# Block transposes on VectorE and a round trip through memory in place of TensorE's transposes, and squares laid out with the summed index innermost, in a Mamba-2 mixer with feed-forward

## The chip, the cores and the metric

The kernel runs on one core of a Trainium2 chip. The metric is the device time of one execution in microseconds, given as the median of several runs. The engines are TensorE (PE, matmuls; PEld is its weight load), VectorE (DVE), ScalarE (ACT), GpSimd (POOL) and SyncE (SP), which in this kernel issues nearly all DMAs. Each engine works through its own queue in order and waits at semaphores.

## The reference

The mixer works on 2 sequences of 512 tokens with 512 channels. The input is projected to a gate, to 8192 channels of heads (128 heads of 64), to B and C (8 groups of 128 states) and to a step size dt for each head. The channels pass a short convolution over 4 tokens and a SiLU. Cut to what matters:

```python
hs = hBC[..., :INTER].reshape(b, s, H, P)
xch = (hs * dt[..., None]).reshape(b, nc, CHUNK, H, P)
Y_diag = jnp.einsum('bzlhn,bzshn,bhzls,bzshp->bzlhp', Cc, Bc, L, xch)
states = jnp.einsum('bzlhn,bhzl,bzlhp->bzhpn', Bc, decay_states, xch)
...
Y = (Y_diag + Y_off).reshape(b, s, H, P) + hs * D[None, None, :, None]
g = y * jax.nn.silu(gate)
gg = g.reshape(b, s, G, INTER // G)
var = jnp.mean(gg * gg, axis=-1, keepdims=True)
gg = gg * jax.lax.rsqrt(var + EPS)
```

An output projection, a residual with layer norm, and a small feed-forward part with low-rank terms and a second layer norm follow. All values are float32.

## The kernel before

**Tiling.** The 1024 tokens are 8 chunks `c` of 128, four to a sequence (`CPB`). The 128 heads are cut into 16 units of 8 heads, 512 channels; a group `g` of B and C has two units, `e` = 0 and 1. A step is (g, e, c), and there are 128. `body(g, last)` on every engine loops over `e` and `c`; the lists `WORK` and `LOOP_TILES` say which weight tiles are projected in which step, 1 to 3 a step and with one or two batches (12 matmuls each), so the next unit's channels are made while this one is worked on. Large operands are split into a high and a low part (`w_hi`, `w_lo`; `xd_hi`, `xd_lo`; `g_hi`, `g_lo`) and multiplied in three float32r matmuls.

**One step.** The channels `hs` have the channel on the partitions. The recurrence needs them with the token on the partitions. So TensorE's `front` (L526) makes four 128x128 transposes into PSUM `p_hid`, and VectorE's `front` (L1210) multiplies by dt into `xdt`. TensorE multiplies `xdt` by the decay matrix into `p_yd` (L690, 8 heads). Right behind `p_yd` stands the front of the next step, then the state update `p_st` (L700 to L702), which needs `xd_hi` and `xd_lo` of the next chunk: GpSimd's `decay_hidden` (L1052, L1054, L1056) makes them from `xdt`. Then comes the output projection of the step before (L562 to L564), which needs its `g_hi` (ACT) and `g_lo` (VectorE).

VectorE adds `y` = `p_yd` + `dh` (L1375), GpSimd multiplies it by the gate (`gate_y`, L1144), ACT squares it into `ysq` (L980) and makes `g_hi`; VectorE sums the squares over the unit's four channel tiles (L1423, L1432), makes `g_lo`, and then `eac` (`scale_off`, L1258) for the next step, which GpSimd adds into `dh` (L1092).

**Queues.** The order in each queue is written out by hand. GpSimd's step is: add `dh`, scale the state (L1097), then for its first tile `split_lo` (`w_lo`, L1034), `gate_y`, `rs`, `skip` (L1063), `decay_hidden` of the next step; then `split_lo` of further tiles. SP's step is: `eac`, `decay`, then for each tile of the step a `raw` load (L388) of the tile four places ahead, which waits until the slot's last content has been split, that is for `w_lo` (and `w_hi`) of the tile two places ahead.

## Time and profile before

| | |
|---|---|
| Median of 3 runs | 1598.37 us (1598.18 to 1598.73) |
| Span of the profiled execution | 1596.2 us |
| TensorE busy | 1577.7 us, 99% |
| VectorE busy | 1347.6 us, 84% |
| ACT busy | 1230.8 us, 77% |
| GpSimd busy | 1224.1 us, 77% |
| DMA | 178.69 MB, mean 112 GB/s |

The span is that of one profiled execution, from the first to the last instruction; the runs' time also holds what lies around it, and the median stands 2.2 us above the span. Busy shares are averages over the whole span; whether an engine sets the time is read from what the others wait for. A matmul's recorded duration overlaps the next one's, so TensorE's times are best read from start to start.

### The profile page before, as it was taken

The numbers are of one execution on the slowest core, as the hardware profiler recorded it, in microseconds if no ns is written. First come the engines' busy times: TensorE is split into PE (matmuls) and PEld (weight loads), VectorE is DVE, ScalarE is ACT, GpSimd is POOL, SyncE is SP. The second block draws the span as 40 slices with busy tenths as digits, with TensorE's granted clock in tenths as the row PEclk, the third lists the DMA queues.
The fourth block names the chain that finished last, engine by engine and source line by source line (L and its number), as shares of the span: only waits on it lengthen the run. The fifth ranks groups of instructions, "written<-read, shape, count | busy, mean of one in ns | idle before, by whom it ended". The sixth has DMA issues, their size and how long they took to land.

```text
span 1596.2 us, 27397 instructions
## 1 busy us (share of the span) xinstructions
PE 1577.7 (99%) x9112; PEld 1299.6 (81%) x9112; DVE 1347.6 (84%) x1878; ACT 1230.8 (77%) x2391; POOL 1224.1 (77%) x1013
## 2 busy tenths in 40 slices
PE   8999999999999999999999999999999999999998
PEld 6878888888888888888888888888888888888865
DVE  6787898879979799787988889887998879978797
ACT  5888778886778877787877877878777886878864
POOL 4578788787797868878687787878688786787864
PEclk9999999999999999999999999999999999999999
DMA  3643424233242322333234332433334333342411
GB/s 116 200 157 108 130 83 153 87 115 108 87 145 96 123 100 100 129 100 109 87 115 140 99 123 74 131 118 92 116 101 136 102 102 106 100 149 77 142 60 60
DMA packets 88156, 178.69 MB, mean 112 GB/s; under 512 B 16592, under 2 KB 20688, under 8 KB 87760
## 3 DMA queue, kind: packets, MB, share of 16 engines
q1 hardware_dynamic: 87008, 176.77, 34.2%
q8 instruction: 74, 1.21, 0.3%
q14 instruction: 66, 0.54, 0.1%
q10 hardware_dynamic: 1008, 0.17, 0.1%
HBM read 172.17 MB, written 4.72 MB: 111 GB/s over the span
## 4 chain that ended last, share of the span: by engine, by line
PE 94%; DVE 1%; POOL 1%; ACT 1%; issue 1%; DMA 0%; SPq 0%; POOLq 0%; DVEq 0%; ACTq 0%
PE proj L514 16%; PE proj L516 16%; PE proj L515 16%; PE p_yd L690 8%; PE p_out L562 7%; PE p_out L564 7%; PE p_out L563 7%; PE p_st L571 5%; PE p_hid L526 4%; PE proj L626 2%; PE p_st L702 1%; PE p_st L700 1%; PE p_st L701 1%; PE p_misc L537 1%; PE p_misc L583 0%
## 5 line engine op out<-in xcount | busy, mean ns | idle before, releaser
L514 PE MATMUL proj<-x_hi,w_hi 128*128 128x512 f32 x1160 | 462.0, 398 | 7.6 <-DVE x_lo L1323 7.0
L515 PE MATMUL proj<-x_lo,w_hi 128*128 128x512 f32 x1160 | 452.9, 390 | 0.0
L516 PE MATMUL proj<-x_hi,w_lo 128*128 128x512 f32 x1160 | 452.9, 390 | 0.0
L1034 POOL TENSOR_TENSOR w_lo<-raw,w_hi 128x512 fp32r<-128x512 f32 x209 | 284.2, 1364 | 101.8 <-ACT w_hi L754 99.3
L1198 DVE SCALAR_TENSOR_TENSOR hs<-proj,uch,hs 128x511 f32<-128x511 f32 (+2 forms) x384 | 285.4, 743 | 42.4 <-ACT hs L781 37.5
L842 ACT ACTIVATE decay<-decay,tok 128x128 f32<-128x128 f32 x1024 | 312.4, 391 | 0.0
L514 PEld LDWEIGHTS proj<-x_hi,w_hi 128*128 128x128 f32 x1160 | 218.8, 189 | 53.2 <-issue 11.2
L516 PEld LDWEIGHTS proj<-x_hi,w_lo 128*128 128x128 f32 x1160 | 218.3, 188 | 46.2
L515 PEld LDWEIGHTS proj<-x_lo,w_hi 128*128 128x128 f32 x1160 | 218.9, 189 | 42.2
L1227 DVE TENSOR_TENSOR decay<-decay,cb 128x1024 f32<-128x1024 f32 x128 | 199.0, 1555 | 56.0 <-ACT decay L860 54.3
L1092 POOL TENSOR_TENSOR dh<-dh,eac 128x512 f32<-128x512 f32 x96 | 127.2, 1325 | 144.0 <-DVE eac L1258 140.3
L1144 POOL TENSOR_TENSOR y<-y,gate 128x512 f32<-128x512 f32 x128 | 180.0, 1406 | 50.3 <-DVE y L1375 50.3
L562 PE MATMUL p_out<-wo_hi,g_hi 128*128 128x512 f32 x512 | 203.6, 398 | 3.3 <-DVE g_lo L1251 3.3
L564 PE MATMUL p_out<-wo_hi,g_lo 128*128 128x512 f32 x512 | 200.1, 391 | 0.0
L563 PE MATMUL p_out<-wo_lo,g_hi 128*128 128x512 f32 x512 | 199.5, 390 | 0.0
L781 ACT ACTIVATE hs<-proj,uch 128x512 f32<-128x512 f32 x128 | 98.6, 773 | 78.8 <-PE proj L516 77.9
L980 ACT ACTIVATE ysq<-y 128x512 f32<-128x512 f32 x128 | 79.9, 624 | 98.8 <-POOL y L1144 98.8
L1375 DVE TENSOR_TENSOR y<-p_yd,dh 128x512 f32<-128x512 f32 x128 | 87.7, 685 | 68.7 <-PE p_yd L690 41.5
L1063 POOL TENSOR_TENSOR dh<-hs,uch 128x512 f32<-128x512 f32 x122 | 145.1, 1189 | 0.0
L754 ACT ACTIVATE w_hi<-raw 128x512 fp32r<-128x512 f32 x197 | 122.8, 623 | 28.2 <-PE proj L516 28.2
L1056 POOL TENSOR_TENSOR xd_lo<-xd,xd_hi 128x512 fp32r<-128x512 f32 x96 | 135.9, 1416 | 7.7
L690 PE MATMUL p_yd<-decay,xdt 128*64 128x128 f32 x2048 | 140.1, 279 | 0.0
(139 smaller groups left out, 3037.6 us busy)
## 6 DMA issues: line engine op xcount, KB each, us to landing
decay<-acum_d SPq DMA_DIRECT2D x128, 512.0 KB, 4.4
raw<-w_t SPq DMA_DIRECT2D x209, 256.0 KB, 2.9
eac<-eacum_d SPq DMA_DIRECT2D x192, 128.0 KB, 3.0
wo_raw<-wo_t SPq DMA_DIRECT2D x32, 256.0 KB, 4.0
c_new<-wo_t SPq DMA_DIRECT2D x32, 256.0 KB, 4.2
hs<-x_t SPq DMA_DIRECT2D x8, 256.0 KB, 5.7
acc<-x_tok SPq DMA_DIRECT2D x8, 256.0 KB, 3.1
out<-acc SPq DMA_DIRECT2D x8, 256.0 KB, 2.0
```

What stands on the lines that cost most here:

```text
L514: nc.tensor.matmul(dst[:], w_hi[:, ws, k, :], x_hi[:, k, cols], start=(k == 0), stop=False)
L515: nc.tensor.matmul(dst[:], w_hi[:, ws, k, :], x_lo[:, k, cols], start=False, stop=False)
L516: mm = nc.tensor.matmul(dst[:], w_lo[:, ws, k, :], x_hi[:, k, cols], start=False, stop=(k == KC - 1))
L562: nc.tensor.matmul(p_out[:], g_hi[:, j, :], wo_hi[:, j, :], start=(j == 0), stop=False)
L563: nc.tensor.matmul(p_out[:], g_hi[:, j, :], wo_lo[:, j, :], start=False, stop=False)
L564: mm = nc.tensor.matmul(p_out[:], g_lo[:, j, :], wo_hi[:, j, :], start=False, stop=(j == UT - 1))
L690: mm = nc.tensor.matmul(p_yd[(h % 2) * HD:(h % 2 + 1) * HD, h // 2, :], xdt[:, h, :], decay[:, dslot(c), h, :], start=True, stop=True)
L842: ins = nc.scalar.activation(decay[:, dslot(c), h, :], decay[:, dslot(c), h, :], ACT.Relu, scale=-1.0, bias=tok[:, e, 0, c, h:h + 1])
L1034: nc.gpsimd.tensor_tensor(w_lo[:, s].rearrange("p a b -> p (a b)"), raw[:, s, :], w_hi[:, s].rearrange("p a b -> p (a b)").bitcast(F32), A ...
L1144: nc.gpsimd.tensor_tensor(y[:], y[:], gate[:, c // CPB, :, (c % CPB) * P:(c % CPB + 1) * P], ALU.mult).then_inc(gated, 1)
L1198: nc.vector.scalar_tensor_tensor(out=dst[:, shift:], in0=src[:, :SEQ - shift], scalar=w, in1=dst[:, shift:], op0=ALU.mult, op1=ALU.add).th ...
L1227: nc.vector.tensor_tensor(decay[:, dslot(c)], decay[:, dslot(c)], bcast(cb[:, c, :], 1, UH), ALU.mult).then_inc(mix_ready, 1)
```

## The change

For the chunks 1 to 7 of a unit the tokens are turned in another way. VectorE's `turn_blocks` transposes the sixteen 32x32 blocks of each partition quadrant (a 32x32 block transpose stays within its 32 partitions) into `x_blk`. SP stores `x_blk` to memory (`turned_d`, `store_blocks`) and loads it back in four DMAs, one for each 32 partitions of `x_tok_sb` (`load_blocks`), which puts the blocks in their places. GpSimd's `scale_tokens` multiplies by dt into `xdt`; for it `lay_dt` copies dt once a unit in the blocks' order. The transposing is done two steps ahead, the product one step ahead. Chunk 0 of each unit still goes by TensorE and `p_hid`. Apart from that, ACT writes the squares with the four channel tiles innermost, so that VectorE's sum reads its input in order. A scratch area for DMA descriptors is set to 1024 bytes.

```diff
@@ SP
+            def store_blocks(g, e, c):
+
+                n = turn_n(g, e, c)
+                sp.wait_ge(blocks_turned, n)
+                wait(sp, x_here, 64 * (n - 2))
+                sp.dma_start(turned_d[n % 2].rearrange("i a n -> (i a) n"),
+                             x_blk[:].rearrange("p q j b -> p (q j b)")).then_inc(blocks_stored, 16)
+
+            def load_blocks(g, e, c):
+
+                n = turn_n(g, e, c)
+                sp.wait_ge(blocks_stored, 16 * n)
+                wait(sp, x_here, 64 * (n - 1))
+                wait(sp, xdt_ready, step(g, e, c) - 1)
+                for q in range(UT):
+                    sp.dma_start(x_tok_sb[q * BLK:(q + 1) * BLK, n % 2].rearrange("a i j b -> a i (j b)"),
+                                 turned_d[n % 2, :, :, q * P:(q + 1) * P].rearrange("i a n -> a i n")).then_inc(x_here, 16)
...
                             load_decay(sp, g + od, ed, cd)
+                        o2, e2, c2 = ahead(e, c, 2)
+                        if c2 and not (last and o2):
+                            store_blocks(g + o2, e2, c2)
                         for t in tiles_of(e, c, last):
...
                                 load_tile(g + off, LOOP_TILES[n], last)
+                        if c2 and not (last and o2):
+                            load_blocks(g + o2, e2, c2)
@@ TensorE, front
-                wait(pe, xdt_ready, step(g, e, c))
-                if c == 0 or c == CPB:
-                    pe.wait_ge(hs_ready, 8 * u + (8 if c else 7 if u else 4))
-                for j in range(UT):
-                    mm = nc.tensor.transpose(p_hid[:, 2 * j:2 * j + 2, :].rearrange("p a b -> p (a b)"),
-                                             hs[:, e, j, c * P:(c + 1) * P], ident[:])
-                mm.then_inc(hid_ready, 1)
+                if c == 0:
+                    wait(pe, xdt_ready, step(g, e, c))
+                    pe.wait_ge(hs_ready, 8 * u + (7 if u else 4))
+                    for j in range(UT):
+                        mm = nc.tensor.transpose(p_hid[:, 2 * j:2 * j + 2, :].rearrange("p a b -> p (a b)"),
+                                                 hs[:, e, j, c * P:(c + 1) * P], ident[:])
+                    mm.then_inc(hid_ready, 1)
@@ ACT
-                        nc.scalar.activation(ysq[:], y[:], ACT.Square).then_inc(sq_ready, 1)
+                        nc.scalar.activation(ysq[:].rearrange("p b a -> p a b"), y[:], ACT.Square).then_inc(sq_ready, 1)
@@ GpSimd
+            def lay_dt(u):
...
+                for r in range(2):
+                    nc.gpsimd.tensor_copy(dt_blk[:, :, r::2, :], tok[:, e, 1].rearrange("p c (j q) -> p c q j", j=UT)).then_inc(dt_blk_ready, 1)
+
+            def scale_tokens(g, e, c):
+
+                pool.wait_ge(x_here, 64 * turn_n(g, e, c))
+                pool.wait_ge(yd_ready, step(g, e, c))
+                if c == 1:
+                    pool.wait_ge(dt_blk_ready, 2 * (2 * g + e + 1))
+                nc.gpsimd.tensor_tensor(xdt[:].rearrange("p h d -> p (h d)").rearrange("p (j i b) -> p i j b", j=UT, i=UT),
+                                        x_tok_sb[:, turn_n(g, e, c) % 2], bcast(dt_blk[:, c], 3, BLK), ALU.mult).then_inc(xdt_ready, 1)
...
                             elif i == 0:
+                                if c < 7:
+                                    scale_tokens(g, e, c + 1)
                                 gate_y(g, e, c)
@@ VectorE
-                nc.vector.tensor_tensor(xdt[:], p_hid[:], bcast(tok[:, e, 1, c, :], 2, HD), ALU.mult).then_inc(xdt_ready, 1)
+                if c == 0:
+                    dve.wait_ge(hid_ready, 2 * g + e + 1)
+                    wait(dve, xd_scaled, carried(g, e, c))
+                    nc.vector.tensor_tensor(xdt[:], p_hid[:], bcast(tok[:, e, 1, c, :], 2, HD), ALU.mult).then_inc(xdt_ready, 1)
...
+            def turn_blocks(g, e, c):
+
+                u = 2 * g + e
+                wait(dve, blocks_stored, 16 * (turn_n(g, e, c) - 1))
+                dve.wait_ge(hs_ready, 8 * u + (8 if c >= CPB else 7 if u else 4))
+                nc.vector.transpose(x_blk[:], hs[:, e, :, c * P:(c + 1) * P].rearrange("p j (q a) -> p q j a", q=UT)
+                                    ).then_inc(blocks_turned, 1)
...
-                        sq_view = ysq[:].rearrange("p a b -> p b a")
...
-                            nc.vector.tensor_reduce(sqs[:, c, :], sq_view, AX.X, ALU.add).then_inc(sqs_ready, 1)
+                            nc.vector.tensor_reduce(sqs[:, c, :], ysq[:], AX.X, ALU.add).then_inc(sqs_ready, 1)
```

SP's queue at the end of a unit, in step e = 1, c = 7, which has two tiles, and at the start of the next step; before:

```order
L366 DMA decay<-acum_d 128x1024 [waits yd_ready]
L388 DMA raw<-w_t 128x512 [waits w_lo_ready,w_hi_ready]
L397 DMA c_new<-wo_t 128x512 [waits wo_lo_ready,wo_hi_ready] x2
L388 DMA raw<-w_t 128x512 [waits w_lo_ready,w_hi_ready]
L355 DMA uch<-unit_chan 128x28
L345 DMA tok<-tok_d 128x192
L351 DMA elast<-elast_d 128x64
L374 DMA eac<-eacum_d 64x512 [waits dh_ready]
```

And now, from the store on:

```order
L396 DMA turned_d<-x_blk 128x512 [waits x_here,blocks_turned]
L416 DMA raw<-w_t 128x512 [waits w_lo_ready,w_hi_ready]
L425 DMA c_new<-wo_t 128x512 [waits wo_lo_ready,wo_hi_ready] x2
L416 DMA raw<-w_t 128x512 [waits w_lo_ready,w_hi_ready]
L406 DMA x_tok_sb<-turned_d 32x4x128 [waits xdt_ready,x_here,blocks_stored]
L406 DMA x_tok_sb<-turned_d 32x4x128 x3
L365 DMA uch<-unit_chan 128x28
L355 DMA tok<-tok_d 128x192
L361 DMA elast<-elast_d 128x64
L384 DMA eac<-eacum_d 64x512 [waits dh_ready]
```

The store has come ahead of the step's raw loads, and the four loads of `x_tok_sb` stand behind the last of them.

GpSimd's queue from the end of a step e = 0, c = 7 on (the last operation of `decay_hidden`, the second tile's `w_lo`, then the step c = 0 of the next unit); before:

```order
L1056 TENSOR_TENSOR xd_lo<-xd,xd_hi 128x512 [waits xdhi_ready]
L1034 TENSOR_TENSOR w_lo<-raw,w_hi 128x512 [waits w_hi_ready] x2
L1144 TENSOR_TENSOR y<-y,gate 128x512 [waits proj_free2,proj_free1,proj_free0,y_ready]
L1063 TENSOR_TENSOR dh<-hs,uch 128x512
L1052 TENSOR_TENSOR xd<-xdt,tok 128x512 [waits st_ready,xdt_ready]
L1054 CAST xd_hi<-xd 128x512 [waits xd_scaled]
L1056 TENSOR_TENSOR xd_lo<-xd,xd_hi 128x512 [waits xdhi_ready]
```

And now:

```order
L1109 TENSOR_TENSOR xd_lo<-xd,xd_hi 128x512 [waits xdhi_ready]
L1069 TENSOR_TENSOR w_lo<-raw,w_hi 128x512 [waits w_hi_ready]
L1087 COPY dt_blk<-tok 128x16x4 [waits xdt_ready]
L1087 COPY dt_blk<-tok 128x16x4
L1069 TENSOR_TENSOR w_lo<-raw,w_hi 128x512 [waits w_hi_ready]
L1095 TENSOR_TENSOR xdt<-x_tok_sb,dt_blk 128x4x4x32 [waits dt_blk_ready,yd_ready,x_here]
L1205 TENSOR_TENSOR y<-y,gate 128x512 [waits proj_free2,proj_free1,proj_free0,y_ready]
L1116 TENSOR_TENSOR dh<-hs,uch 128x512
L1105 TENSOR_TENSOR xd<-xdt,tok 128x512 [waits st_ready,xdt_ready]
L1107 CAST xd_hi<-xd 128x512 [waits xd_scaled]
L1109 TENSOR_TENSOR xd_lo<-xd,xd_hi 128x512 [waits xdhi_ready]
```

The two copies of `lay_dt` stand between the two `w_lo`, and the product into `xdt` for c = 1 has come ahead of the gate of c = 0; it waits for the four loads.

TensorE's queue from `p_yd` on, in a step of e = 0; before:

```order
L690 MATMUL p_yd<-decay,xdt 64x128 x7
L526 MATMUL p_hid<-ident,hs 128x128 [waits xdt_ready]
L526 MATMUL p_hid<-ident,hs 128x128 x3
L537 MATMUL p_misc<-cT,bT 128x128 [waits cb_taken]
L700 MATMUL p_st<-xd_hi,b_hi 128x512 [waits yoff_scaled,xd_ready]
```

And now:

```order
L725 MATMUL p_yd<-decay,xdt 64x128 x7
L572 MATMUL p_misc<-cT,bT 128x128 [waits cb_taken]
L735 MATMUL p_st<-xd_hi,b_hi 128x512 [waits yoff_scaled,xd_ready]
L736 MATMUL p_st<-xd_lo,b_hi 128x512
L737 MATMUL p_st<-xd_hi,b_lo 128x512
```

The four transposes are gone, and `p_st` comes that much sooner after `p_yd`.

## Rows read from the trace of the kernel before

**Rows 1.** The page, part 1: busy us (share of the span) xinstructions.

```profile
PE 1577.7 (99%) x9112; PEld 1299.6 (81%) x9112; DVE 1347.6 (84%) x1878; ACT 1230.8 (77%) x2391; POOL 1224.1 (77%) x1013
```

**Rows 2.** The page, part 4: the chain that ended last, by engine.

```profile
PE 94%; DVE 1%; POOL 1%; ACT 1%; issue 1%; DMA 0%; SPq 0%; POOLq 0%; DVEq 0%; ACTq 0%
```

**Rows 3.** Windows of two units: PE, PEld, DVE, ACT, POOL busy us, PEclk, DMA share, GB/s.

```profile
640.20:730.40 90.20, 90.20 (x537) 74.57 (x539) 75.21 (x103) 73.05 (x143) 73.02 (x59) 1.00 0.35 113
730.40:830.80 100.40, 100.40 (x581) 83.93 (x582) 88.95 (x121) 76.15 (x148) 78.01 (x65) 1.00 0.34 107
```

**Rows 4.** Timeline of TensorE: start us, us, engine line op tiles.

```profile
605.14 0.66 PE L526 MATMUL p_hid<-ident,hs 128*128 128x128 f32 x4
605.55 0.47 PE L700 MATMUL p_st<-xd_hi,b_hi 128*128 128x512 f32 x1
...
641.12 0.66 PE L526 MATMUL p_hid<-ident,hs 128*128 128x128 f32 x4
641.61 0.39 PE L537 MATMUL p_misc<-cT,bT 128*128 128x128 f32 x2
```

**Rows 5.** Groups by line: busy us, mean ns of one | idle before.

```profile
L1052 POOL TENSOR_TENSOR xd<-xdt,tok 128x512 f32<-128x512 f32 x96 | 135.0, 1406 | 0.6 <-DVE xdt L1210 0.6
...
L1210 DVE TENSOR_TENSOR xdt<-p_hid,tok 128x512 f32<-128x512 f32 x128 | 87.1, 680 | 0.0
...
L980 ACT ACTIVATE ysq<-y 128x512 f32<-128x512 f32 x128 | 79.9, 624 | 98.8 <-POOL y L1144 98.8
...
L1423 DVE TENSOR_REDUCE sqs<-ysq 128x128 f32<-128x512 f32 x64 | 69.1, 1079 | 5.1 <-ACT ysq L980 5.1
```

**Rows 6.** Timeline of GpSimd (POOL), 640 to 784 us.

```profile
640.47 2.53 POOL L1034 TENSOR_TENSOR w_lo<-raw,w_hi 128x512 fp32r<-128x512 f32 x2
642.96 1.28 POOL L1144 TENSOR_TENSOR y<-y,gate 128x512 f32<-128x512 f32 x1
...
645.72 1.04 POOL L1052 TENSOR_TENSOR xd<-xdt,tok 128x512 f32<-128x512 f32 x1
...
648.40 1.29 POOL L1056 TENSOR_TENSOR xd_lo<-xd,xd_hi 128x512 fp32r<-128x512 f32 x1
...
651.36 1.27 POOL L1092 TENSOR_TENSOR dh<-dh,eac 128x512 f32<-128x512 f32 x1
...
707.86 1.31 POOL L1056 TENSOR_TENSOR xd_lo<-xd,xd_hi 128x512 fp32r<-128x512 f32 x1
...
782.14 1.28 POOL L1056 TENSOR_TENSOR xd_lo<-xd,xd_hi 128x512 fp32r<-128x512 f32 x1
```

**Rows 7.** The chain in order of time: start us, us, what.

```profile
640.16 1.02 PE p_yd L690 x16
...
652.00 1.02 PE p_yd L690 x16
...
708.96 1.02 PE p_yd L690 x16
...
783.12 1.02 PE p_yd L690 x16
```

**Rows 8.** Timeline of SP's queue at the same place.

```profile
641.82 0.33 SPq L388 DMA_DIRECT2D raw<-w_t  x1
...
642.67 0.42 SPq L345 DMA_DIRECT2D tok<-tok_d  x1
643.14 0.43 SPq L351 DMA_DIRECT2D elast<-elast_d  x1
```

**Rows 9.** The page, part 6: DMA issues, KB each, median us to landing.

```profile
raw<-w_t SPq DMA_DIRECT2D x209, 256.0 KB, 2.9
eac<-eacum_d SPq DMA_DIRECT2D x192, 128.0 KB, 3.0
...
out<-acc SPq DMA_DIRECT2D x8, 256.0 KB, 2.0
...
elast<-elast_d SPq DMA_DIRECT2D x16, 32.0 KB, 3.8
```

More of the change, by code:

```diff
@@ L35 @@
 EPS = 1e-5
+BLK = 32
 HALVES = (slice(0, HID // 2), slice(HID // 2, HID))
@@ L128, in mixer_ffn_kernel @@
         xdt = sb("xdt", [P, UH, HD])
+        x_blk = sb("x_blk", [P, UT, UT, BLK])
+        x_tok_sb = sb("x_tok_sb", [P, 2, UT, UT, BLK])
+        dt_blk = sb("dt_blk", [P, CHUNKS, UT, UT])
         xd = sb("xd", [P, UH, HD])
@@ L132, in mixer_ffn_kernel @@
         y = sb("y", [P, UT, P])
-        ysq = sb("ysq", [P, UT, P])
+        ysq = sb("ysq", [P, P, UT])
         g_hi, g_lo = sb("g_hi", [P, UT, P], F32R), sb("g_lo", [P, UT, P], F32R)
@@ L259, in decay_round, with turn_n @@
             return 8 * g + (4 * e + c // 2 + 1) if c % 2 else 4 * g + (2 * e + c // 4 + 1)
+        def turn_n(g, e, c):
+            return 7 * (2 * g + e) + c
         def tile_n(g, t):
@@ L461, in _ @@
             sp.wait_ge(tok_here, 1)
+            store_blocks(0, 0, 1)
+            load_blocks(0, 0, 1)
             def body(g, last):
@@ L1043, in split_both @@
                 split_lo(g, t)
+            def lay_dt(u):
+                g, e = u // 2, u % 2
+                if g:
+                    pool.wait_ge(unit_loaded[e], 48 * g + 32)
+                wait(pool, xdt_ready, 8 * u)
+                for r in range(2):
[7 more added lines that the diff above has]
+                                        x_tok_sb[:, turn_n(g, e, c) % 2], bcast(dt_blk[:, c], 3, BLK), ALU.mult).then_inc(xdt_ready, 1)
             def decay_hidden(g, e, c):
@@ L1078, in _ @@
             pool.wait_ge(tok_here, 1)
+            lay_dt(0)
             decay_hidden(0, 0, 0)
@@ L1105, in body @@
                             if i == 0 and (g, e, c) == (0, 0, 0):
+                                scale_tokens(0, 0, 1)
                                 decay_hidden(0, 0, 1)
@@ L1117, in body @@
                         if not tiles:
-                            if c == 7:
+                            if c < 7:
+                                scale_tokens(g, e, c + 1)
+                            else:
                                 lagged_rms(g, e, c)
@@ L1126, in body @@
                                     skip(g + off, ne, ncn)
+                        if c == 7 and not (last and off):
+                            lay_dt(2 * g + e + 1)
                         if last and e == 1 and c >= 5:
@@ L1206, in front @@
             def front(g, e, c):
-                dve.wait_ge(hid_ready, step(g, e, c) + 1)
-                wait(dve, xd_scaled, carried(g, e, c))
-                nc.vector.tensor_tensor(xdt[:], p_hid[:], bcast(tok[:, e, 1, c, :], 2, HD), ALU.mult).then_inc(xdt_ready, 1)
+                if c == 0:
+                    dve.wait_ge(hid_ready, 2 * g + e + 1)
+                    wait(dve, xd_scaled, carried(g, e, c))
+                    nc.vector.tensor_tensor(xdt[:], p_hid[:], bcast(tok[:, e, 1, c, :], 2, HD), ALU.mult).then_inc(xdt_ready, 1)
                 if e == 0:
@@ L1344, in _ @@
             front(0, 0, 0)
+            turn_blocks(0, 0, 1)
             mix(0, 0, 0)
@@ L1389, in body @@
                             front(g + off, ne, ncn)
+                        o2, e2, c2 = ahead(e, c, 2)
+                        if c2 and not (last and o2):
+                            turn_blocks(g + o2, e2, c2)
                         if tiles:
@@ L1426, in body @@
                                 ln_stats_2(*ln)
-                            nc.vector.tensor_reduce(last_sqs(c), sq_view, AX.X, ALU.add).then_inc(sqs_ready, 1)
+                            nc.vector.tensor_reduce(last_sqs(c), ysq[:], AX.X, ALU.add).then_inc(sqs_ready, 1)
                         else:
                             wait(dve, sqs_ready, s)
-                            nc.vector.tensor_tensor(ysq[:, 0, :], ysq[:, 0, :], sqs[:, c, :], ALU.add).then_inc(sqt_ready, 1)
+                            nc.vector.tensor_tensor(ysq[:, :, 0], ysq[:, :, 0], sqs[:, c, :], ALU.add).then_inc(sqt_ready, 1)
                             dve.wait_ge(sqt_ready, 8 * g + c + 1)
-                            nc.vector.tensor_reduce(sqs[:, c, :], sq_view, AX.X, ALU.add).then_inc(sqs_ready, 1)
+                            nc.vector.tensor_reduce(sqs[:, c, :], ysq[:], AX.X, ALU.add).then_inc(sqs_ready, 1)
                         for ln in lns:
@@ L1531 @@
     }
-    nc = bacc.Bacc("TRN2", target_bir_lowering=False, num_devices=1)
+    nc = bacc.Bacc("TRN2", target_bir_lowering=False, num_devices=1, dynamic_dma_scratch_size=1024)
     ins = [nc.dram_tensor(k, a.shape, mybir.dt.from_np(a.dtype), kind="ExternalInput").ap() for k, a in arrays.items()]
```

2 lines of the change are left out of this document (added).

## The prediction

> **What bounds the kernel now.** I read the page first: TensorE is busy 99% of the span, VectorE 84%, ACT and GpSimd (POOL) 77% each [rows 1]. The chain of waits then says whether that busy time is the path: 94% of the chain that ended last is TensorE work [rows 2]. So a matmul taken from TensorE's queue is worth its full time, as long as the other engines keep up. To see whether they can, I took one unit (eight steps) at a time from the table of windows: with e = 0 it lasts 90.2 us, GpSimd is busy 73.0 of them and VectorE 75.2; with e = 1 it lasts 100.4 us, with GpSimd at 78.0 and VectorE at 89.0; the granted clock is 1.00 in both, the upper level, 2.4 GHz [rows 3]. GpSimd has 17.2 and 22.4 us to spare in a unit. The change puts work on exactly this engine, so it is there that the answer lies.
>
> **What is removed from TensorE.** 7 of every 8 steps lose the four transposes into p_hid, 112 of 128 steps. Their records are 0.66 us long, but they overlap what follows, so I take start to start: 605.14 to 605.55 is 0.41 us where p_st comes next, and 641.12 to 641.61 is 0.49 us where p_misc comes next (e = 0) [rows 4]. A group sheds 7 x 0.49 + 7 x 0.41 = 6.3 us, eight groups 50 us. That is the whole gain there can be.
>
> **VectorE.** The product xdt (680 ns) becomes a block transpose over the same 512 elements. No row shows one. Bounds: what it replaces, 680 ns, and the slowest one-input row of this size, the strided reduction at 1079 ns [rows 5]; it reads runs of 32 elements, so I take 0.7. The reduction over ysq then reads in order; 680 ns is the nearest row, 1079 if the stride wasn't the cause; I take 0.7, so 128 x 0.38 = 49 us come off VectorE. It isn't on the path, so this buys cover, not time. ACT's Square (624 ns [rows 5]) now writes every element 16 bytes from the last. No row has such a write; it costs nothing more, or up to the same factor as the strided read, 1079/680, which is 0.37 us. The squares reach VectorE's reduction later by as much as the reduction gets shorter, and g_lo behind it starts when it did. I take nothing for this pair of edits; without the shorter reduction the 0.37 us would lie in the loop gate, square, g_lo, eac.
>
> A rule that speaks against this pair: the Trainium skill, SBUF — State Buffer, section Door 1: The DMA port swizzle, says that SBUF is accessed in 16-byte lines, that the full rate needs two or more accesses in a line, and that each one that crosses into a new line pays. The 1079 ns reduction agrees as to reads; by the same page the Square gets slower. The sum is the same with the page as without it.
>
> **GpSimd.** It takes over the product, 112 times. Its bounds are 1.3 us, the bare gate product (642.96), and 1.41 us, the mean of xd, which sometimes waits beside VectorE [rows 5, 6]. I take 1.3: 9.1 us in a unit, and 16 times two copies of 64 elements for dt_blk, near 0.25 us each, hidden behind the wait below. A unit of e = 0 then holds 82.6 us of GpSimd work in 90.2 - 3.4 = 86.8 us. On average it fits. What does not is the order.
>
> **The new wait.** In SP's queue the four loads of x_tok_sb stand behind every raw load of the step, and the last raw load of a step with two tiles waits for a w_lo that GpSimd makes at the end of that step (the SP rows in the change section). At the turn from e = 1 to e = 0 this can be laid out. Time 0 is the end of p_yd, 640.16 + 1.02 = 641.18 [rows 7]. The first of the two w_lo that start at 640.47 ends at +0.55 [rows 6]. SP sends raw (0.33 us), then four loads 0.48 us apart, as uch, tok and elast are [rows 8]: the last goes out at +2.5. No row has such a load (64 KB, pieces of 512 B). The nearest are raw and eac at 2.9 and 3.0 us; the ends are out at 2.0 and elast, in 256 B pieces, at 3.8 [rows 9]. I take 3.0. The blocks are there at +5.5; GpSimd was ready for them at +1.8 (before) or +2.3 (with dt_blk). From there: product +6.8, gate +8.1, rs and skip +9.5 (642.96 to 645.72 is 2.76 for the three, less gate), the three xd operations +13.5 (645.72 to 649.69 is 4.0 [rows 6]). The matmuls into p_st want them right after p_yd and p_misc of the next step: before at 653.0 + 0.5, that is +12.3, now +11.8. TensorE waits 1.7 us.
>
> GpSimd has no pause left behind that: w_lo and dh (1.3 each [rows 6]), state and a second w_lo, some 5 us; then it stands once more for loads that were sent only after the first of these w_lo (end +14.8, so the last load lands near +19.7). Carried on in the same way, the next xd set ends near +28 where TensorE wants it at +27.5 (0.4 us lost); g_lo then comes just in time. At c = 4 and c = 6 there is no load to wait for, but the product itself stands in front of xd: before, xd for c = 6 ended at 709.17 and p_yd at 709.98, a spare of 0.8, and 0.3 more for p_misc; less 1.3 for the product and 0.4 for the shorter step it is short by 0.6, and c = 4 I take the same [rows 6, 7]. Sum for e = 0: 1.7 + 0.4 + 0.6 + 0.6 = 3.3 us, all of the 3.4 us shed. For e = 1: 1.2 us at c = 1 in the same way, 0.6 at c = 4, where xd ended at 783.42 and p_yd at 784.14 [rows 6, 7]; the long step of c = 1 (four batches) lets GpSimd catch up. 1.8 of 2.9 us are lost. A group gains 0.1 + 1.1 = 1.2 us, eight of them 10 us.
>
> **The store** I take as hidden: VectorE transposes two steps ahead, by my estimate 4 us after p_yd; store (2 to 3 us [rows 9]), four issues and landing follow, so in a one-tile step the blocks are there some 11 us after p_yd, about when GpSimd asks in the next step. SP is told to wait for the transpose ahead of raw; raw has a step to spare. eac and decay go out up to 2 us later; they are awaited by a step that is itself later then. The product from p_hid at c = 0 stays as it was. The last group, with fewer tiles, is taken like the others.
>
> **The sum.** The profiled execution had 1596.2 us; 1596.2 - 50 + 40 = 1586. The median of the runs is 2.2 us above that span, so 1588.
>
> **Rivals.**
> First, *the loads are in time*. If a load lands in 2.0 us instead of 3.0, every stand of GpSimd gets 1 us shorter. Such a microsecond counts three times in a unit of e = 0 (c = 0, 1, 2, since GpSimd is never idle between) and once in e = 1: 4 us in a group, 32 in all. 1588 - 32 = 1556; with no wait at all 1548. For it: the out rows [rows 9] and VectorE's lighter load. Against it: out is a store, and the loads of weights and eac into SBUF took 2.9 and 3.0. The Trainium skill, DMA: Bandwidth & Descriptors, section Anatomy of one DMA, gives a fixed 2.0 us and 436 GB/s, measured on GpSimd's path, which is 2.15 us for 64 KB; by that page the time would be an estimated 1561. This trace doesn't agree: its 256 KB loads take 2.9 us where the page gives 2.6.
>
> Second, on the other side, *the loads land later*, as elast does at 3.8 us [rows 9], because its pieces are small, or because four DMAs onto 32 partitions each follow one another. Then 0.8 x 4 x 8 = 26 us are added: 1614. It decides from a landing of 3.4 us on (0.4 x 32 = 13 us, the gain of 10 and the 0.2%).
>
> Third, *the product is dearer*: at the 2.0 us that xd takes when VectorE reads two SBUF tensors beside it, 0.7 us more in some six steps a group gives 34 us, 1622. For it: VectorE's mix runs near the same time; against it: the mean of xd is 1.41.
>
> **The numbers.** My forecast (GpSimd's stands eat most of the gain, 1575 to 1602) 0.43, the loads in time 0.25, the loads late 0.25, a dearer product or transpose 0.07. About 0.2% (3 us) is what a measurement tells from no change. Of the first case's 0.43, 0.33 lie below 1595, 0.10 within; so faster 0.58, same 0.10, slower 0.32. The range goes from the case of no waits, 1548, to the third rival, 1620.
>
> **What would show it.** Right: p_hid's matmuls 64 instead of 512, p_yd to p_st closer by 0.4 us; GpSimd near 87% busy, idle ahead of the product at c = 1 and c = 2 with the load of x_tok_sb named as releaser; TensorE's weight load for p_st waiting for xd_lo, 25 us or more in all. Wrong: a product that waits for p_yd only, or a p_st that never waits (then the first rival); VectorE's transpose at twice 0.7 us, so that y is late; a load that lands in over 3.4 us.

## The result and the profile after

The changed kernel takes 1675.97 us (median of 4 runs, 1672.36 to 1678.27) against 1598.46 of the kernel before beside it: ratio 1.0485, 95% interval 1.0470 to 1.0499. It is slower by 77.5 us, outside the predicted range.

The page of the changed kernel, parts 1 and 4 (busy us, share of the span, instructions; then the chain that ended last), where before it had [rows 1, 2]:

```profile
PE 1565.3 (94%) x8664; PEld 1268.4 (76%) x8664; DVE 1363.0 (81%) x1878; ACT 1278.9 (76%) x2391; POOL 1367.4 (82%) x1157
...
PE 27%; POOL 19%; issue 18%; DVE 18%; ACT 14%; DMA 2%; SPq 1%; ACTq 0%; DVEq 0%; POOLq 0%
```

TensorE was 94% of the chain of waits that ended last and is 27%. It now stands (has nothing to do) for 108 us of the 1673.6 us span (18.5 us before). Its 8664 matmuls take 1565.3 us, though 448 transposes are gone (9112 less 8664).

The changed kernel's groups by line (busy us, mean ns of one | idle before, releaser), for [rows 5]:

```profile
L1205 POOL TENSOR_TENSOR y<-y,gate 128x512 f32<-128x512 f32 x128 | 189.9, 1484 | 11.1 <-DVE y L1446 11.1
L1015 ACT ACTIVATE ysq<-y 128x512 f32<-128x512 f32 x128 | 146.1, 1141 | 203.0 <-POOL y L1205 203.0
L1095 POOL TENSOR_TENSOR xdt<-x_tok_sb,dt_blk 128x512 f32<-128x512 f32 x112 | 124.4, 1110 | 59.7 <-DMA x_tok_sb<-turned_d 59.6
L1290 DVE STREAM_TRANSPOSE x_blk<-hs 128x512 f32<-128x512 f32 x112 | 78.4, 700 | 2.5 <-DMA turned_d<-x_blk 2.5
L1496 DVE TENSOR_REDUCE sqs<-ysq 128x128 f32<-128x512 f32 x64 | 43.4, 678 | 46.2 <-ACT ysq L1015 45.3
```

Its DMA issues (KB each, median us to landing), for [rows 9]:

```profile
raw<-w_t SPq DMA_DIRECT2D x209, 256.0 KB, 2.8
turned_d<-x_blk SPq DMA_DIRECT2D x112, 256.0 KB, 2.4
x_tok_sb<-turned_d SPq DMA_DIRECT2D x448, 64.0 KB, 2.1
```

And what its TensorE waited for (us in total, times, longest):

```profile
PE p_st L735 <- DVE eac L1328: 30.7, 16, 3.1
PE p_misc L572 <- DVE var L1309: 18.0, 11, 2.1
PE p_st L735 <- POOL xd_lo L1109: 17.6, 23, 1.8
```

The transpose (700 ns), the sum (678 ns) and the product (1110 ns) cost what was taken or less, and a load lands in 2.1 us where 3.0 was taken. GpSimd nevertheless stands 59.6 us for those loads, and ACT's Square waits 203 us for the gate product where it waited 98.8 us before [rows 5]. TensorE waits more for VectorE's results (eac, var) than for xd.

### The profile page after: what moved, and what is told of

It is laid out like the page before. It is cut to its first block, busy times and chain, and to the rows that moved or that the text cites. A ratio compares the mean times of both kernels' runs of the same rounds, so it can differ in the third digit from the quotient of the medians.

```text
span 1673.6 us, 27534 instructions
## 1 busy us (share of the span) xinstructions
PE 1565.3 (94%) x8664; PEld 1268.4 (76%) x8664; DVE 1363.0 (81%) x1878; ACT 1278.9 (76%) x2391; POOL 1367.4 (82%) x1157
## 4 chain that ended last, share of the span: by engine, by line
PE 27%; POOL 19%; issue 18%; DVE 18%; ACT 14%; DMA 2%; SPq 1%; ACTq 0%; DVEq 0%; POOLq 0%
PE proj L549 6%; DVE hs L1259 6%; PE proj L550 6%; PE proj L551 6%; POOL y L1205 5%; ACT decay L877 3%; POOL w_lo L1069 3%; DVE g_lo L1321 3%; POOL dh L1116 2%; POOL xdt L1095 2%; ACT ysq L1015 2%; ACT w_hi L789 2%; DVE ysq L1503 2%; ACT decay L895 2%; POOL xd L1105 2%
## 5 line engine op out<-in xcount | busy, mean ns | idle before, releaser
L1069 POOL TENSOR_TENSOR w_lo<-raw,w_hi 128x512 fp32r<-128x512 f32 x209 | 290.7, 1392 | 45.2 <-ACT w_hi L789 41.8
L1015 ACT ACTIVATE ysq<-y 128x512 f32<-128x512 f32 x128 | 146.1, 1141 | 203.0 <-POOL y L1205 203.0
L1297 DVE TENSOR_TENSOR decay<-decay,cb 128x1024 f32<-128x1024 f32 x128 | 207.1, 1618 | 45.7 <-ACT decay L895 45.7
L597 PE MATMUL p_out<-wo_hi,g_hi 128*128 128x512 f32 x512 | 207.8, 406 | 9.4 <-issue 5.0
L1205 POOL TENSOR_TENSOR y<-y,gate 128x512 f32<-128x512 f32 x128 | 189.9, 1484 | 11.1 <-DVE y L1446 11.1
L1095 POOL TENSOR_TENSOR xdt<-x_tok_sb,dt_blk 128x512 f32<-128x512 f32 x112 | 124.4, 1110 | 59.7 <-DMA x_tok_sb<-turned_d 59.6
L1116 POOL TENSOR_TENSOR dh<-hs,uch 128x512 f32<-128x512 f32 x122 | 153.0, 1254 | 0.0
L1321 DVE TENSOR_TENSOR g_lo<-y,g_hi 128x512 fp32r<-128x512 f32 x128 | 141.3, 1104 | 3.5 <-ACT g_hi L884 2.6
```

Of the source, the lines that this page charges most:

```text
L597: nc.tensor.matmul(p_out[:], g_hi[:, j, :], wo_hi[:, j, :], start=(j == 0), stop=False)
L1069: nc.gpsimd.tensor_tensor(w_lo[:, s].rearrange("p a b -> p (a b)"), raw[:, s, :], w_hi[:, s].rearrange("p a b -> p (a b)").bitcast(F32), A ...
L1205: nc.gpsimd.tensor_tensor(y[:], y[:], gate[:, c // CPB, :, (c % CPB) * P:(c % CPB + 1) * P], ALU.mult).then_inc(gated, 1)
L1297: nc.vector.tensor_tensor(decay[:, dslot(c)], decay[:, dslot(c)], bcast(cb[:, c, :], 1, UH), ALU.mult).then_inc(mix_ready, 1)
L1321: nc.vector.tensor_tensor(g_lo[:].rearrange("p a b -> p (a b)"), y[:].rearrange("p a b -> p (a b)"), g_hi[:].rearrange("p a b -> p (a b)") ...
```

## Where the time goes, step by step

Below, worked out from the starts of p_yd in the traces, is the time from one step's p_yd to the next's, for the third of the eight groups of each profiled execution. The experiments named here (e4 to e13) are told further down; the sums are from start to start.

```
                            e=0: c=0   1    2    3    4    5    6    7 | e=1: 0    1    2    3    4    5    6    7   sum
before                         11.8 14.5 11.6 10.1 11.7  9.0 11.6  9.8 |  11.4 19.9 11.5  9.9 11.7 14.2 11.5 10.2  190.7
e4 no transposes               11.5 15.1 11.2  9.7 11.3  8.6 12.3  9.8 |  11.0 20.3 11.1  9.5 12.4 13.9 11.1 10.3  189.3
e11 e4 + GpSimd product        11.5 14.4 11.2  9.7 11.3  8.6 12.6  9.8 |  11.1 21.2 11.1  9.5 13.0 13.9 11.1 11.7  191.9
e12 before + GpSimd product    11.8 14.4 11.6 10.1 11.7  9.0 11.9  9.8 |  11.4 20.9 11.5  9.9 12.2 14.2 11.5 11.1  193.3
e5 blocks, no round trip       11.5 14.3 11.2  9.7 11.3  8.6 12.6  9.8 |  11.0 21.5 11.1  9.5 12.9 14.0 11.1 11.7  192.0
e7 loads early                 11.5 14.3 11.2  9.7 11.3  8.6 12.6  9.8 |  11.0 23.6 11.1  9.5 13.0 13.9 11.1 11.7  194.1
e13 e7 + early w_lo            11.5 14.3 11.2  9.7 11.3  8.6 12.6  9.8 |  11.0 21.5 11.1  9.5 13.0 13.9 11.1 11.7  192.1
changed kernel                 11.5 16.8 11.2 10.0 13.2  8.7 12.9  9.8 |  11.6 23.7 11.1  9.5 12.7 13.9 11.1 12.0  199.9
```

Steps that only shed the transposes get 0.3 to 0.4 us shorter. The others lose more than that at a few places: in the changed kernel at c = 1, 4 and 6 of e = 0, and at c = 1, 4 and 7 of e = 1.

One such place, the turn that the prediction laid out [rows 6, 7], in the changed kernel: first SP's queue, then GpSimd's timeline.

```profile
669.10 0.33 SPq L416 DMA_DIRECT2D raw<-w_t  x1
669.53 1.80 SPq L406 DMA_DIRECT2D x_tok_sb<-turned_d  x4
...
669.34 1.29 POOL L1069 TENSOR_TENSOR w_lo<-raw,w_hi 128x512 fp32r<-128x512 f32 x1
673.32 1.05 POOL L1095 TENSOR_TENSOR xdt<-x_tok_sb,dt_blk 128x512 f32<-128x512 f32 x1 [2.68 <-DMA x_tok_sb<-turned_d]
674.33 2.25 POOL L1205 TENSOR_TENSOR y<-y,gate 128x512 f32<-128x512 f32 x1
...
680.21 1.27 POOL L1109 TENSOR_TENSOR xd_lo<-xd,xd_hi 128x512 fp32r<-128x512 f32 x1
```

p_yd began at 667.91, so time 0 of the prediction's walk is 668.93. The product starts at +4.4 (predicted +5.5) and xd is set at +12.5 (predicted +13.5): the walk is right to a microsecond. Part of that is luck. The loads landed 0.9 us sooner than taken, the product took 1.05 us for 1.3 and the three xd operations 3.4 us for 4.0, while the gate product took 2.25 us for 1.3. But look at who holds TensorE in that step. Its timeline, and VectorE's:

```profile
679.38 1.09 PE L725 MATMUL p_yd<-decay,xdt 128*64 128x128 f32 x16
682.24 0.46 PE L572 MATMUL p_misc<-cT,bT 128*128 128x128 f32 x2 [1.77 <-DVE var L1309]
...
677.78 0.69 DVE L1496 TENSOR_REDUCE sqs<-ysq 128x128 f32<-128x512 f32 x1 [2.33 <-ACT ysq L1015]
678.39 1.27 DVE L1321 TENSOR_TENSOR g_lo<-y,g_hi 128x512 fp32r<-128x512 f32 x1
679.58 0.68 DVE L1328 TENSOR_TENSOR eac<-p_st,eac 128x512 f32<-128x512 f32 x1
680.18 0.67 DVE L1303 TENSOR_TENSOR half<-half,p_out 128x512 f32<-128x512 f32 x1
680.77 1.25 DVE L1315 SCALAR_TENSOR_TENSOR wo_lo<-wo_raw,uch,wo_hi 128x512 fp32r<-128x512 f32 x1
681.95 0.15 DVE L1309 TENSOR_SCALAR var<-p_misc 128x1 f32<-128x1 f32 x1
```

What comes last here isn't xd. The product stands ahead of the gate, so the gate is late by the stand and the product; the Square behind it is late, VectorE stands 2.33 us for the Square, and var, which frees p_misc, comes 1.77 us after TensorE wants it. By then xd is there too (681.48); alone it would have held TensorE for some 0.7 us, an estimate from p_st's start 0.35 us behind p_misc's in the step before. The prediction followed one consumer of GpSimd's queue, and there were three.

The stands for the loads lie elsewhere than the walk had them. Of the 59.6 us, 23 are in step c = 0 of e = 0 and 21 in c = 0 of e = 1, near 2.6 us each time (3.2 by the prediction's own figures for e = 0); the second stand, in the step behind it, isn't there (0.2 us, once), and short ones come at c = 2 of e = 0 (0.7 us) and c = 6 of e = 1 (0.5 to 2.1 us).

## The experiments

Theory A: ACT's strided Square is what costs. Theory B: GpSimd's work is, the product and its wait. B has two halves. Theory C: GpSimd's stands for the four loads, which are behind the step's last raw load, are the main loss. Theory D: the product has no place in GpSimd's queue, in time or not. The median of the kernel before was 1598.2 to 1598.7 us beside all of these runs.

**The two parts apart.** e1 is the kernel before with the squares' layout alone (the lines of the diff above on ysq); e2 is the changed kernel without it.

> The kernel before with the layout of the squares alone (ACT writes them 16 bytes apart, VectorE sums in order). Theory A (the strided write is the main cost: in the changed kernel the Square took 1141 ns and not 624, and it stands in the loop gate, square, g_hi, g_lo, eac, dh): the Square at 1141 here too, ScalarE 66 us busier, and the time 10 to 60 us above the kernel before. Theory B (GpSimd's product and its wait for the loads are the main cost, the squares a bystander): within 5 us of the kernel before, since the sum gets 0.4 us shorter where the Square gets 0.5 us longer.

> The changed kernel with the squares laid out as before: block transposes, store, four loads and the product on GpSimd stay. Theory A: most of the 78 us go, and the time is 1585 to 1610, near what the prediction gave for the blocks alone (1588). Theory B: 1650 or more, and GpSimd's pauses for x_tok_sb stay near 60 us.

e1: 1604.37 us, ratio 1.0038 (1.0023 to 1.0053). e2: 1669.69 us, 1.0447 (1.0431 to 1.0462). So the layout costs 6 us alone and 6 us on top of the blocks. That is a little above what theory B gave e1 and below what A gave it; e2 came as B had it. In e1 the Square takes 1136 ns where it took 624 [rows 5], and the sum 677 where it took 1079:

```profile
L980 ACT ACTIVATE ysq<-y 128x512 f32<-128x512 f32 x128 | 145.4, 1136 | 101.3 <-POOL y L1144 101.3
...
L1422 DVE TENSOR_REDUCE sqs<-ysq 128x128 f32<-128x512 f32 x64 | 43.3, 677 | 7.7 <-ACT ysq L980 6.7
```

Theory A is out as the main cause. The write costs 0.51 us more, past the prediction's bound of 0.37, and the sum gives back 0.40. The Trainium skill, SBUF — State Buffer, section Door 1: The DMA port swizzle, has each access that crosses into a new 16-byte line pay; both rows agree with it.

**What the shorter sum is worth.** e3 is the kernel before with the squares summed in the order in which they lie (other elements than the reference's are summed):

```diff
-sq_view = ysq[:].rearrange("p a b -> p b a")
+sq_view = ysq[:].rearrange("p a b -> p (a b)").rearrange("p (b a) -> p b a", a=UT)
```

> The kernel before; the sum reads the naturally laid squares in order, so it adds other elements than the variance needs (only the time is of use). ScalarE's Square as before. It measures what the shorter reduction alone is worth. Both theories: the reduction near 680 ns and not 1079, VectorE 49 us less busy, and a time 0 to 5 us lower, since TensorE is busy 99% of the span already.

1595.55 us, 0.9983 (0.9973 to 0.9992). The sums got 52 us shorter, but VectorE's busy time fell by 28.5 us only (1347.6 to 1319.1, where 49 were expected): most of the rest went to g_lo right behind them. Before, then e3:

```profile
L1251 DVE TENSOR_TENSOR g_lo<-y,g_hi 128x512 fp32r<-128x512 f32 x128 | 107.5, 840 | 1.3 <-ACT g_hi L849 1.3
...
L1251 DVE TENSOR_TENSOR g_lo<-y,g_hi 128x512 fp32r<-128x512 f32 x128 | 127.0, 993 | 1.7 <-ACT g_hi L849 1.7
```

The same g_lo takes 982 ns in e1. The time gained is 3 us.

**What the transposes are worth.** e4 is the kernel before without TensorE's transposes for c = 1 to 7; nothing takes their place, so xdt is made from old values. e9 is e4 with e3's sum.

```diff
-                for j in range(UT):
+                if c == 0:
+                    for j in range(UT):
...
-                dve.wait_ge(hid_ready, step(g, e, c) + 1)
+                dve.wait_ge(hid_ready, 2 * g + e + 1)
```

> The kernel before without TensorE's transposes for the chunks 1 to 7; VectorE's product reads what chunk 0 left in p_hid (the hidden values of the other chunks are left out of the computation). It measures the gain that was shed from TensorE with nothing put in its place. The prediction's term: 50 us, so 1548. If VectorE, ScalarE and GpSimd can't follow a shorter step even unloaded, less: 1560 to 1580.

> The kernel before without TensorE's transposes for c = 1 to 7 (nothing in their place, so xdt is made from what stands in p_hid) and with the sum of squares read in order (wrong elements are summed). Without the transposes alone the time was 1587.5 us, with the sum in order alone 1595.6. If the shed time is lost because VectorE is late (eac, var, g_lo), 112 x 0.33 = 37 us of matmul time come closer to being kept and it is 1570 to 1580. If VectorE has nothing to do with it, both effects add up at most: 1584 to 1585.

e4: 1587.55 us, 0.9933 (0.9916 to 0.9949), above both of the expectations. e9: 1581.75 us, 0.9898 (0.9882 to 0.9915), between its two. With the other queues as they are, the whole gain there can be is 11 us, not 50. TensorE's busy time falls by 36.9 us, 0.33 us a step, and its idle time rises from 18.5 to 45. The waits of e4's TensorE:

```profile
PE p_st L701 <- DVE eac L1259: 7.8, 9, 1.2
...
PE p_misc L538 <- DVE var L1240: 5.8, 6, 1.0
```

In the table, e4 loses what it shed at four steps (c = 1 and 6; c = 1 and 4): these get 2.3 us longer in a group, the others 3.7 us shorter. VectorE seems to be part of this, a small one: e9 is 16.4 us below the kernel before, 2.9 us more than the two effects alone add up to (10.7 and 2.7), which is no more than the three intervals leave open. What else takes the rest of the 37 us isn't parted further.

**The loads.** e5 is e2 with the blocks stored and loaded once, at the start, and every product made from that set. e7 is e2 with the four loads behind the step's first raw load, which changes only the steps with two or three tiles. e6 is e2 with the gate ahead of the product, and e8 is e6 and e7 together. The edits of e7 and e6, cut:

```diff
+                        blocks_due = c2 and not (last and o2)
                         for t in tiles_of(e, c, last):
...
+                            if blocks_due:
+                                load_blocks(g + o2, e2, c2)
+                                blocks_due = False
...
```

```diff
-                                if c < 7:
-                                    scale_tokens(g, e, c + 1)
                                 gate_y(g, e, c)
+                                if c < 7:
+                                    scale_tokens(g, e, c + 1)
```

> e2 without the round trip for each chunk: the blocks are stored and loaded once at the start, and every product reads that one set (so the hidden values are left out; VectorE's transposes and GpSimd's product stay). The reference points are e2 at 1669.7 us and e4, without transposes and without anything in their place, at 1587.6. Theory C (GpSimd waits for the loads; the lag is never made up): most of the 82 us between them go, 1600 to 1620. Theory D (the product itself, 1.1 us more in a GpSimd queue that has no slack at the turns of the units, and gate_y behind it): 1635 to 1665, with GpSimd's busy time as in e2 (1377 us).

> e2 with the product behind gate_y in GpSimd's queue, ahead of the rest. If what costs is that the gate (and so the square, g_hi, g_lo and eac) stands behind the product and its loads, ScalarE's wait for the gate falls from 222 us towards the 108 of e4, and the time to 1620 to 1645. If it is xd that is late, no change or 5 us slower, since xd comes no earlier.

> e2 with the four loads behind the first raw load of a step and not behind the last. GpSimd's waits for x_tok_sb (55 us, up to 4.0 each) should go to under 10. Theory C: 1610 to 1635. Theory D: 1650 to 1662, some 10 to 20 us less at most. If the wait for the store now holds up the second raw load, ScalarE's w_hi waits for raw and part of it is lost.

> e6 and e7 together on e2. If the two costs are independent, the gains add up; if both lie on the same GpSimd chain at the turn of the units, it is the better of the two and little more. I expect 1610 to 1640, still slower than the kernel before (1598).

e5: 1615.76 us, 1.0110 (1.0095 to 1.0125). e6: 1656.99, 1.0369 (1.0354 to 1.0384). e7: 1618.37, 1.0116 (1.0086 to 1.0145). e8: 1631.22, 1.0208 (1.0193 to 1.0223). The round trip costs 54 us, and four loads in another place of SP's queue give back 51 of them, with the same bytes and nearly the same landing (2.0 us). The 51 is good to some 5 us, as e7's four runs spread from 1611.7 to 1622.2 us; the two shorter ones had a mean granted clock of 0.997, the two longer ones 0.992 and 0.991. Theory C holds for this part. What C doesn't explain is the rest: e5 and e7, without a stand worth the name (e7's GpSimd waits 6.4 us for the loads), are 18 and 20 us above the kernel before and 28 and 31 above e4. Putting the gate first helps by 13 us while the loads are late, less than its expectation of 25 or more: the gate fills part of the stand (29.0 us of it are left of e2's 54.7). With the loads early it costs 13 us, and TensorE waits 21.4 us for xd_lo where it waited 15.3 in e7.

e2 also shows how the three consumers share the wait when the squares lie as before:

```profile
PE p_st L735 <- POOL xd_lo L1109: 36.2, 33, 2.2
PE p_misc L572 <- DVE var L1309: 15.2, 9, 2.3
...
PE p_st L735 <- DVE eac L1328: 3.2, 1, 3.2
```

p_st needs both xd_lo and the bank that eac frees, and the profile names the later. Here that is xd, as the prediction had it; in the changed kernel the longer Square makes it eac (30.7 us against 17.6). That the two paths end so close to each other may be why the layout adds only 6 us.

**The product.** e10 is e7 with the product on VectorE, in its old place. e11 is e4, and e12 the kernel before, with an unused GpSimd product at the product's place, in 111 steps (the first step of all has none). Both also set the scratch area for descriptors to 1024 bytes, as the change does; no run has that alone, but e12's steps without a loss take what the kernel before takes, to 0.03 us.

```diff
+            def extra(g, e, c):
+                pool.wait_ge(yd_ready, step(g, e, c))
+                nc.gpsimd.tensor_tensor(spare[:], spare[:], spare[:], ALU.mult)
```

> The blocks turned as in the change, the four loads issued behind the step's first raw load (1618.4 us when alone) and the product with dt on VectorE, where it stood before the change, instead of on GpSimd. Theory D (GpSimd has no room for 112 products of 1.1 us in front of xd): GpSimd is as free as before the change, about 28 us come back, less what 0.7 us more a step on VectorE cost: 1590 to 1605. Rival (the transposes or their wait are what costs): VectorE is busy 90% and y and g_lo are late, 1615 or more.

> The kernel without TensorE's transposes (1587.5 us; nothing in their place) plus one GpSimd product over 128x512 on a tensor that nobody else uses, at the place where the change puts the product with dt, in 112 steps. No step waits for its data. Theory D (GpSimd's time): 1610 to 1620, as with blocks loaded only once (1615.8). Rival (what costs is that xd now waits for a product of GpSimd's own, or the transposes on VectorE): 1588 to 1595.

> The kernel before, whole, plus the same unused GpSimd product in 112 steps. GpSimd would be busy 84 to 86% of the time. If its room of 17 to 22 us in a unit can be used (the prediction's 'on average it fits'), 1598 to 1601. If the room doesn't lie where the steps need it, 1605 to 1620; the difference to the run without transposes then says what the shorter TensorE step has to do with it.

e11: 1607.99 us, 1.0062 (1.0047 to 1.0077), 20.4 above e4 and just under theory D's range. e12: 1616.90 us, 1.0117 (1.0102 to 1.0132), 18.7 above the kernel before. So 1.1 us of GpSimd work a step whose data nobody waits for, at this place of the queue, costs 19 to 20 us, with the transposes or without. Theory D holds for 20 of the 28 us.

The other 8 (e5 less e11) are no steady cost of the block transposes: in the table e5 and e11 take the same time for a group, 192.0 and 191.9 us. 4 us lie in the first two steps of the first group (29.9 against 25.8 us), the rest mostly in the long step of groups 5 and 7 (23.6 against 21.2 us). And 45 matmuls over 512 columns start 0.41 to 0.44 us behind the one before in e5, 11 in e11; the others do so after 0.23 us. That makes 7 of the 8 us (34 times 0.2, an estimate from the two traces), with mean granted clocks of 0.993 and 1.000. Why the clock falls in e5 and not in e11 is open.

e12's page, and its unused product:

```profile
PE 1582.2 (98%) x9112; PEld 1299.0 (80%) x9112; DVE 1375.3 (85%) x1878; ACT 1228.9 (76%) x2391; POOL 1375.8 (85%) x1125
...
L1049 POOL TENSOR_TENSOR spare<-spare 128x512 f32<-128x512 f32 x111 | 120.5, 1085 | 0.0
```

GpSimd is 85% busy there and the time is lost all the same. The product also makes others longer: GpSimd's busy time rises by 151.7 us for 120.5 of product (xd took 1406 ns and takes 1575), and VectorE's by 27.7 us with no work added.

e10: 1626.45 us, 1.0178 (1.0163 to 1.0193), 8 us worse than e7. The expectation's rival was right: VectorE goes to 91% busy, its product from two SBUF tensors takes 1173 ns where the one from p_hid took 680, and TensorE waits for eac:

```profile
L1278 DVE TENSOR_TENSOR xdt<-x_tok_sb,dt_blk 128x512 f32<-128x512 f32 x112 | 131.3, 1173 | 7.6 <-DMA x_tok_sb<-turned_d 7.0
```

```profile
PE p_st L739 <- DVE eac L1335: 16.3, 16, 1.5
```

In the middle groups e10 (193.3 us) is no worse than e7; the 5.5 us between the two profiled executions lie in the first and the last group.

**The long step.** In the table e7's step e = 1, c = 1 takes 23.6 us instead of 19.9. Its TensorE and GpSimd there:

```profile
756.52 0.39 PE L555 MATMUL proj<-x_hi,w_lo 128*128 128x512 f32 x1
758.76 0.47 PE L553 MATMUL proj<-x_hi,w_hi 128*128 128x512 f32 x1 [1.85 <-issue]
...
761.11 0.63 PE L555 MATMUL proj<-x_hi,w_lo 128*128 128x512 f32 x1
761.53 0.63 PE L553 MATMUL proj<-x_hi,w_hi 128*128 128x512 f32 x1
...
756.95 1.71 POOL L1073 TENSOR_TENSOR w_lo<-raw,w_hi 128x512 fp32r<-128x512 f32 x1
```

The profile names no releaser ("issue"), but w_lo ends at 758.66 and TensorE goes on at 758.76. Theory E: TensorE stands there for this w_lo, its clock falls behind the stand, and without the stand most of the loss goes. e13 is e7 with this w_lo ahead of dh and state; e14 is the kernel before with that order; e15 is the whole change with both reorderings.

```diff
+                        early = (e, c) == (1, 1) and split_after(e, c, 0, last)
+                        if early:
+                            split_lo(g + early[0], early[1])
                         if c % CPB:
...
-                            if nxt:
+                            if nxt and not (early and i == 0):
                                 split_lo(g + nxt[0], nxt[1])
```

> The blocks turned as in the change, squares as before, the four loads behind the step's first raw load (1618.4 us) and, in step e = 1, c = 1 of each group, GpSimd makes w_lo of the third tile (B) ahead of dh and the state, some 3 us sooner. Theory E (TensorE waits there for this w_lo, and its clock falls behind the stand): the 1.85 us stand goes and with it the 1.6 us of slower matmuls, 8 x 3.5 = 28 us: 1590 to 1600, and the mean granted clock rises from 0.992. Rival (another release, or the stand moves on to y or p_out, since dh and the state come 1.7 us later): 1610 to 1620.

> The kernel before with the same order of w_lo, dh and state in step e = 1, c = 1. TensorE doesn't stand there in the kernel before, so theory E expects 1597 to 1599. A gain of 3 us or more would mean that this order is worth something without the change, and the gain of the run beside it would have to be read less that.

> The whole change, squares' layout included, with the four loads behind the first raw load and the early w_lo. If the effects add up, it is the time of the run without the squares' layout plus 6 us: near 1600 by theory E, near 1620 by the rival.

e13: 1612.52 us, 1.0083 (1.0068 to 1.0098), 5.9 below e7. e14: 1596.90 us, 0.9988 (0.9979 to 0.9998). e15: 1621.08 us, 1.0140 (1.0123 to 1.0157). Theory E is right about the release: that stand is gone, and no matmul behind it is slow (granted clock 1.00 over the step; mean clock of the run 0.998 after 0.992). It is wrong about the worth. The step comes to 21.5 us, not to 20, because TensorE now stands for 1.38 us ahead of the next projection, which needs the next w_lo:

```profile
763.29 0.47 PE L553 MATMUL proj<-x_hi,w_hi 128*128 128x512 f32 x1 [1.38 <-issue]
...
761.92 2.52 POOL L1073 TENSOR_TENSOR w_lo<-raw,w_hi 128x512 fp32r<-128x512 f32 x2
```

And not every group of e7 had lost 3.7 us there (the step took 23.6 us in three of them, 20.7 to 22.0 in four others). The 5.9 us are themselves not clear of the noise, as e7's and e13's intervals overlap and e7's fastest run (1611.7 us) is below e13's median. By the count used above, 54 matmuls of the profiled e7 start at the slow distance and 20 of e13, which is an estimated 7 us: between these two executions most of what e13 gains is the clock. e15 stands 8.6 us above e13 and 55 us below the changed kernel. No version with the blocks turned beats the kernel before. The other order of w_lo alone (e14) is 1.8 us below it, so of e13's 5.9 us some 2 may have nothing to do with the change.

## Why the prediction was wrong

The forecast was 1588 us, 10 below the kernel before. Step by step from the kernel before to the changed one: 1598.3; transposes gone, -10.7 (e4); a GpSimd product in the queue, +20.4 (e11); the product on real data with VectorE's transposes, +7.8 (e5), most of it TensorE's clock; the loads' round trip, +53.9 (e2); the squares' layout, +6.3 (the changed kernel). That is 1676.0. Each term is the difference of two runs in a row, so the terms add up by construction. Where another order was run it gave nearly the same: 18.7 for the product on the kernel before (e12), 6.1 for the layout (e1).

- **"So a matmul taken from TensorE's queue is worth its full time, as long as the other engines keep up": the first step that failed.** 50 us were entered; 37 came off TensorE's busy time (0.33 us a step, where 0.41 and 0.49 were read from start to start), and 10.7 off the kernel. The others did not keep up even with nothing added to them. TensorE at 99% said that little made it wait in the kernel before, not that nothing stood right behind it.
- **"On average it fits. What does not is the order.": the second.** The order was seen, but the room was taken as usable wherever the walk found no wait. 17 us of room in a unit did not take 8 us of work: e12 has no round trip at all and loses 18.7 us.
- **The new wait: its mechanism was right, its size was not.** GpSimd is idle ahead of the product with the load named (59.6 us in 33 waits), and the loads were sent only behind the raw load that waits for w_lo. The 40 us of losses for loads and product together measured 82 (20.4 + 7.8 + 53.9). By steps of the table, with 0.33 us shed a step: e = 0 was to lose 3.3 us a group and lost some 6; e = 1 was to lose 1.8 and lost some 8, 4 of them in the long step, of which the prediction said that it lets GpSimd catch up. In the changed kernel TensorE stands there for eac (2.0 us at 776.71), in e7 for w_lo.
- **A slip in the walk.** For e = 1, c = 4 the prediction has 0.6 us. Its own terms, 0.7 of spare less 1.3 and 0.4, leave it short by 1.0: in e = 1 no p_misc stands ahead of p_st, as the kernel before shows. With it the forecast would have been some 3 us later, still far from the result.

```profile
784.08 0.66 PE L526 MATMUL p_hid<-ident,hs 128*128 128x128 f32 x4
784.49 0.47 PE L700 MATMUL p_st<-xd_hi,b_hi 128*128 128x512 f32 x1
```

- **What the walk left out.** It followed xd alone, and in the laid-out turn TensorE waited 1.77 us for var. A late GpSimd holds TensorE by three ways: xd; gate, Square, sums, then g_lo, eac and var; and w_lo. In the changed kernel the first holds it for 17.6 us and eac and var for 48.7 us; with the squares as before (e2) it is 36.2 and 18.4 us. The third is what e7 and e13 show.
- **What the clock took.** No term of the sum had it. 87 matmuls of the changed kernel start at the slow distance and 17 of e4, an estimated 14 us (last section).
- **"I take nothing for this pair of edits" (the squares): wrong, +6 us.** The write was past its bound, and the prediction's own sentence on the loop (gate, square, g_lo) named where it would lie.
- **Rivals.** The loads in time: a landing of 2.1 us did come, and the gain it was to bring did not, as the place in SP's queue, not the landing, made the wait. The Trainium skill, DMA: Bandwidth & Descriptors, section Anatomy of one DMA, gives an estimated 2.15 us for 64 KB; the 2.1 us here agree. For raw's 256 KB it gives 2.6 us, and 2.8 was measured; the page's fit is for GpSimd's path. The loads late: no. The product dearer: no, 1.11 us, though the gate behind it now often meets VectorE's decay product (2.25 us at 674.33, 1.28 at 642.96 before [rows 6]).
- **What was right:** transpose 700 ns, sum 678 ns, p_hid's matmuls cut to 64, the xd walk to 1 us (with offsetting errors), and the store as hidden: e7, with store and early loads, is within 3 us of e5 without them. TensorE's weight load for p_st does wait for xd_lo, but 23.6 us where "25 us or more" was written, and GpSimd is 82% busy where 87% was: its 1367 us are spread over a longer span.

## What to carry to other kernels

Before work is taken from the busiest engine, take it out alone, with nothing in its place: that bounds the gain, and here it was a fifth of what the busy share promised. Before work is given to an engine with room, put the same work there on a tensor that nobody uses, at the same place of its queue; here a share of 77% said nothing of the room at that place. When a queue gets later, list everything that is taken from behind the new instruction, and follow each to the engine that sets the time; and a DMA issue behind a wait in SP's queue is as late as that wait, however fast it lands.
